# Layer 0 of a two-layer fp32 transformer: keys and values by seven half-size products, head dimension on partitions, turned by block transposes and memory

## What is computed

```
qkv  = silu(x @ qkv_w.T)            # per head q, k, v: 1024 x 128
for each chunk of tokens:
    scores = (q @ k.T) * diag_decay
    out    = scores @ v + (q * q_decay) @ state
    state  = state * chunk_decay + (k * k_decay).T @ v
xf   = out / sqrt(mean(out^2) + eps)
x    = layernorm(x + (sigmoid(x @ gate_w.T) * norm_w * xf) @ out_w.T)
```

## Time and profile before

| | us |
|---|---|
| median of three runs | 3062.18 (3061.16 to 3062.97) |
| profiled execution | 3054.36 |
| its span | 3052.4 |
| PE busy in the span | 2927.9 (96%) |
| DVE, ACT, POOL busy | 2027.4, 1544.3, 1740.4 |
| layer 0, head loop | until about 1112 |

### The profile page before, as it was taken

How to read it: one execution, slowest core, us unless ns; L and a number is a source line. 1 busy time by engine, 2 the same in 40 slices (tenths; PEclk the granted TensorE clock), 3 DMA queues, 4 the chain that set the end, 5 groups by cost and what they waited for, 6 DMA issues and landing times. The chain is left out here.

```text
span 3052.4 us, 57532 instructions
## 1 busy us (share of the span) xinstructions
PE 2927.9 (96%) x17440; PEld 2630.0 (86%) x17440; DVE 2027.4 (66%) x3231; ACT 1544.3 (51%) x3019; POOL 1740.4 (57%) x1300
## 2 busy tenths in 40 slices
PE   7999999999999978899999999999999999986998
PEld 6999999999999957799989899898989999975886
DVE  5555656555565556677777777777777777775555
ACT  4443443344344323566666666666666666663222
POOL 5554554455455432466665666666666666654664
PEclk9999999999999989999999999999999999998999
DMA  3222222222222220456666565665656666566541
GB/s 114 66 77 86 65 66 85 78 65 74 86 68 65 71 73 23 153 194 208 197 201 207 192 204 195 205 204 197 203 192 205 199 204 202 193 197 185 153 141 45
DMA packets 310074, 430.57 MB, mean 141 GB/s; under 512 B 30464, under 2 KB 237312, under 8 KB 309888
## 3 DMA queue, kind: packets, MB, share of 16 engines
q1 hardware_dynamic: 272336, 294.82, 32.5%
q10 hardware_dynamic: 37680, 135.02, 11.1%
HBM read 276.63 MB, written 153.09 MB: 141 GB/s over the span
## 5 line engine op out<-in xcount | busy, mean ns | idle before, releaser
L1588 ACT ACTIVATE b_prob<-b_s_ps,b_shift 128x1024 f32<-128x1024 f32 x256 | 285.7, 1116 | 345.9 <-DVE b_shift L1738 338.7
L82 PE MATMUL b_pj_kq<-b_w_hi,xT_hi 128*128 128x384 f32 x1008 | 351.7, 349 | 23.8 <-DVE b_nat L1714 22.5
L83 PE MATMUL b_pj_kq<-b_w_lo,xT_hi 128*128 128x384 f32 x1008 | 342.8, 340 | 0.0
L84 PE MATMUL b_pj_kq<-b_w_hi,xT_lo 128*128 128x384 f32 x1008 | 342.6, 340 | 0.0
L1744 DVE STREAM_TRANSPOSE b_blocks<-b_prob 128x1024 f32<-128x1024 f32 x256 | 317.4, 1240 | 29.0 <-ACT b_prob L1588 28.5
L489 POOL TENSOR_TENSOR a_ga_lo<-a_gated,a_ga_hi 128x512 fp32r<-128x512 f32 x64 | 112.8, 1763 | 366.7 <-ACT a_ga_hi L577 366.7
L1510 POOL TENSOR_TENSOR b_pT_lo<-b_pT_lo,b_pT_hi 128x1024 fp32r<-128x1024 f32 x128 | 304.9, 2404 | 18.7 <-ACT b_pT_hi L1577 18.6
L1510 POOL TENSOR_TENSOR pT_lo<-pT_lo,pT_hi 128x1024 fp32r<-128x1024 f32 x128 | 305.0, 2406 | 13.1 <-ACT pT_hi L1577 13.1
L1495 POOL TENSOR_TENSOR b_rstd<-b_mean_sq,power 128x4 f32<-128x4 f32 x128 | 128.8, 1007 | 320.1 <-DVE b_mean_sq L1724 313.5
L1738 DVE TENSOR_REDUCE b_shift<-b_s_ps 128x1 f32<-128x1024 f32 x256 | 307.1, 1200 | 1.7 <-PE b_s_ps L84 1.7
L82 PE MATMUL a_pj<-b_w_hi,xT_hi 128*128 128x256 f32 x1024 | 295.5, 289 | 13.2 <-DVE xT_lo L825 11.0
(11 more groups left out here) (302 smaller groups left out, 9149.3 us busy)
## 6 DMA issues: line engine op xcount, KB each, us to landing
bounce<-b_blocks ACTq DMA_DIRECT2D x256, 512.0 KB, 3.5
pT_lo<-bounce SPq DMA_DIRECT2D x512, 128.0 KB, 3.1
b_pT_lo<-bounce SPq DMA_DIRECT2D x512, 128.0 KB, 2.9
b_w_raw<-in_w SPq DMA_DIRECT2D x32, 768.0 KB, 5.8
b_w_raw<-in_w SPq DMA_DIRECT2D x95, 256.0 KB, 3.2
k_bounce<-a_k_blocks SPq DMA_DIRECT2D x32, 512.0 KB, 4.0
a_k_raw<-k_bounce SPq DMA_DIRECT2D x128, 128.0 KB, 2.9
a_w_raw<-in_w SPq DMA_DIRECT2D x32, 256.0 KB, 3.1
```

The costliest lines, as they stand in the source:

```text
L82: pe.matmul(out, w_hi, x_hi, start=first, stop=False, skip_group_check=partial)
L83: pe.matmul(out, w_hi, x_lo, start=False, stop=False, skip_group_check=partial)
L84: return pe.matmul(out, w_lo, x_hi, start=False, stop=last, skip_group_check=partial)
L1588: act.activation(prob[t % 2][:, :], s_ps[t % 2][:, :], ACT.Exp, bias=shift[:, t:t + 1], accum_out=row_sum[:, t:t + 1]).then_inc(exp_done, 1)
```

## The change

Keys and values are now also made by seven half-size products, at s = 0 to 3, with key weights as first and value weights as second row of the scheme (`PARTS`, pair `KV`; gate and queries are pair `QG`). Their weights get sums and partial splits of their own, on POOL and ACT at s = 4 to 6 of step h for head h+2. Keys and values come out with the head dimension on partitions, so the scores use `k_T` as it stands; both are turned to tokens on partitions for the updates and outputs: two block transposes, four writes to memory of 256 KB, one read of 1 MB, and ACT's `copy_v`. `decay_k` reads the moved blocks. At the start, the sums and splits of x are put in another order and the token sums are made earlier. The core of the diff:

```diff
 # SP
             def load_weights(h, t):
-                wait(sp, w_lo_done, NW * (h - 1) + (K_W + 1, V_W + 1, NW, NW)[t])
-                sp.dma_start(w_raw[t][:, :, :], w[ds(h, 1), t].rearrange("a p k d -> (a p) k d")).then_inc(w_in[t], 16)
+                wait(sp, w_lo_done, NW * (h - 1) + (L_S4, NW)[t // 2])
+                sp.dma_start(w_raw[t][:, :, :], w[ds(h, 1), t].rearrange("a p k d -> (a p) k d")).then_inc(
+                    w_in[t // 2], 16)
-            def move_k(g):
-                sp.wait_ge(k_blocked, g + 1)
-                sp.dma_start(k_bounce[:, :, :, :].rearrange("r p c n -> (r p) (c n)"),
-                             k_blocks[:, :, :, :].rearrange("p c t x -> p (c t x)")).then_inc(k_moved, 16)
-                sp.wait_ge(k_moved, MOVED * g + 16)
+            def move_kv(g):
+                sp.wait_ge(kv_blocked, 2 * g + 2)
                 for c in range(GROUPS):
-                    sp.dma_start(k_raw[c * BLK:(c + 1) * BLK].rearrange("p r t x -> p r (t x)"),
-                                 k_bounce[:, :, c, :].rearrange("r p n -> p r n")).then_inc(k_moved, 16)
+                    sp.dma_start(kv_bounce[:, :, c, :].rearrange("r x n -> x r n"),
+                                 kv_blocks[c * BLK:(c + 1) * BLK].rearrange("p r k t y -> p r (k t y)")).then_inc(
+                        kv_moved, 16)
+                sp.wait_ge(kv_moved, MOVED * g + WRITTEN)
+                wait(sp, v_copied, 2 * g)
+                wait(sp, k_decayed, 2 * g)
+                sp.dma_start(kv_raw[:, :, :, :, :].rearrange("p c k t y -> p (c k t y)"),
+                             kv_bounce[:, :, :, :].rearrange("r x c n -> (r x) (c n)")).then_inc(kv_moved, 16)
             def load(h, b):
                 load_weights(h, 0)
                 load_weights(h, 1)
                 load_output_weights(h - 2)
-                move_k(h - 2)
+                move_kv(h - 2)
                 load_weights(h, 2)
                 load_weights(h, 3)
                 load_decays(h - 1, 1 - b)
 # POOL, in step(h, ...), place s (at s == 6 half_out(h, b, 0) stands ahead of this)
-                    if split and s in SPLITS:
-                        split_lo(h + 2, SPLITS[s])
+                    for at, pair, g in ((s, QG, h + 1), (s - 4, KV, h + 2)):
+                        if (project, split)[pair == KV] and 0 <= at < 3:
+                            if at == 0:
+                                weight_sums(g, pair)
+                            for n in STAGES[at]:
+                                weight_low(g, pair, n)
 # STAGES = ((L_A1,), (L_S12, L_A22), (L_S3, L_S4)); weight_low(g, pair, n) waits for weight_high's of the same n
 # ACT
-            def copy_k(h, b, j):
...
+            def copy_v(h, j):
+                act.wait_ge(kv_moved, MOVED * (h + 1))
+                wait(act, attn, 2 * (h - 1) + j + 1)
+                cut = slice(CH * j, CH * (j + 1))
+                act.activation(v_nat[:, cut, :].rearrange("p t (c y) -> p t c y", y=BLK),
+                               kv_raw[:, :, 1, cut, :].rearrange("p c t y -> p t c y"), ACT.Copy).then_inc(v_copied, 1)
             def decay_k(h, b, j):
-                act.wait_ge(silu, 6 * h + 2 * j + 2)
+                act.wait_ge(kv_moved, MOVED * (h + 1))
...
+            def keep_first(g, bg, pair):
+                act.wait_ge(proj, NP * g + len(ORDER) * pair + P1)
+                wait(act, *((kv_blocked, 2 * g), (attn, 2 * (g - 1)))[pair])
+                act.activation(second(pair, bg)[:, 0:HALF], pj[pair][:, :], ACT.Copy).then_inc(kept, 1)
             def step(h, b, attention, project, output, split):
                 for s in range(NG):
                     if attention:
                         if s in (0, 2):
-                            copy_k(h, b, s // 2)
+                            copy_v(h, s // 2)
                             decay_k(h, b, s // 2)
...
+                    if project:
+                        sigmoids(h + 1, 1 - b, s)
+                    for at, pair, g in ((s, QG, h + 1), (s - 4, KV, h + 2)):
+                        if (project, split)[pair == KV] and 0 <= at < 3:
+                            for n in STAGES[at]:
+                                weight_high(g, pair, n)
 # PE
-                    if project and s < KV.stop:
-                        project_group(h + 1, s)
-                    if project and s >= KV.stop:
-                        for p in PRODUCTS[s]:
-                            product(h + 1, p)
+                    if project:
+                        for p in PRODUCTS[s % 4]:
+                            product(h + 1, s // 4, p)
 # in product(g, pair, p)
+                if p == P2:
+                    pe.wait_ge(kept, 2 * g + pair + 1)
 # DVE
+                    if project and s == 4:
+                        blocks(h + 1, 1 - b, 0)
+                        blocks(h + 1, 1 - b, 1)
+                    if project:
+                        projected(h + 1, 1 - b, s)
```

More of the change, by code:

```diff
@@ L434, in _ @@
             pool.memset(sh.power[:, :], -0.5).then_inc(zeroed, 1)
[L435 to L466, removed]
+            def raw(pair, row, cut):
+                return w_raw[PARTS[pair][row]][:, cut, :]
+            def weight_sums(g, pair):
+                pool.wait_ge(w_in[pair], 32 * (g + 1))
+                wait(pool, proj, NP * (g - 1) + len(ORDER) * (pair + 1))
+                to = {n: s_raw[pair][:, cut, :] for n, cut in in_s.items()}
+                done = 8 * g + 4 * pair
+                pool.tensor_tensor(to[S1], raw(pair, 1, LOWER), raw(pair, 1, UPPER), ALU.add).then_inc(w_summed, 1)
+                pool.tensor_tensor(to[S3], raw(pair, 0, LOWER), raw(pair, 1, LOWER), ALU.subtract).then_inc(w_summed, 1)
+                pool.wait_ge(w_summed, done + S1)
+                pool.tensor_tensor(to[S2], to[S1], raw(pair, 0, LOWER), ALU.subtract).then_inc(w_summed, 1)
+                pool.wait_ge(w_summed, done + S2)
+                pool.tensor_tensor(to[S4], raw(pair, 0, UPPER), to[S2], ALU.subtract).then_inc(w_summed, 1)
@@ L536, in _, with weight_high, tokens_high @@
         def _(act):
[L537 to L542, removed]
+            act.dma_start(w_raw[V_W][:, :, :], w[0, V_W]).then_inc(w_in[KV], 16)
             for k in (2, 3):
                 act.dma_start(xT_raw[k][:, 0:HALF], xT[k * P:(k + 1) * P, 0:HALF]).then_inc(x_in[0][k], 16)
[L545 to L548, removed]
+            def weight_high(g, pair, n):
+                act.wait_ge(w_in[pair], 32 * (g + 1))
+                wait(act, proj, NP * (g - 1) + len(ORDER) * (pair + 1))
+                if n == L_A1:
+                    t = PARTS[pair][0]
+                    hi, from_ = w_hi[t][:, :, :], w_raw[t][:, :, :]
+                elif n == L_A22:
+                    t = PARTS[pair][1]
+                    hi, from_ = w_hi[t][:, UPPER, :], w_raw[t][:, UPPER, :]
+                else:
+                    cut = {L_S12: slice(0, 4), L_S3: in_s[S3], L_S4: in_s[S4]}[n]
+                    hi, from_ = s_hi[pair][:, cut, :], s_raw[pair][:, cut, :]
+                    act.wait_ge(w_summed, 8 * g + 4 * pair + {L_S12: S2, L_S3: S3, L_S4: S4}[n])
+                act.activation(hi, from_, ACT.Copy).then_inc(w_hi_done, 1)
+            def tokens_high(*which):
+                for j, k in which:
                     cut = slice(j * HALF, (j + 1) * HALF)
@@ L593, in token_sums_high @@
-            def token_sums_high(*which):
-                for n in which:
-                    act.wait_ge(x_summed, 2 * n + 2)
-                    act.activation(t_hi[n], t_raw[n], ACT.Copy).then_inc(x_hi_done, 1)
-            def sigmoid(g, bg, s):
-                act.wait_ge(proj, NP * g + s + 1)
-                half = s % 2
-                wait(act, silu, 6 * g + s - 1 if s >= 2 else 6 * (g - 1) + 6 - s)
-                act.activation(sig_tmp[half][:, :], pj[half][:, :], ACT.Sigmoid).then_inc(sig, 1)
@@ L621, in query_sigmoid, with second @@
-            def query_sigmoid(g, bg, half):
-                act.wait_ge(combined, NC * g + (C21, C22)[half])
-                wait(act, silu, 6 * g + 3 + half)
-                act.activation(sig_tmp[half][:, :], q_T[bg][:, half * HALF:(half + 1) * HALF],
-                               ACT.Sigmoid).then_inc(sig, 1)
+            def second(pair, bg):
+                return (v_T, q_T[bg])[pair]
+            def keep_first(g, bg, pair):
+                act.wait_ge(proj, NP * g + len(ORDER) * pair + P1)
+                wait(act, *((kv_blocked, 2 * g), (attn, 2 * (g - 1)))[pair])
+                act.activation(second(pair, bg)[:, 0:HALF], pj[pair][:, :], ACT.Copy).then_inc(kept, 1)
@@ new lines, in sigmoid, with sigmoids @@
+            def sigmoid(g, silu_index, from_):
+                wait(act, silu, 6 * g + silu_index - 2)
+                act.activation(sig_tmp[(silu_index - 1) % 2][:, :], from_, ACT.Sigmoid).then_inc(sig, 1)
+            def sigmoids(g, bg, s):
+                pair = s // 4
```

(60 more changed lines are left out.)

315 lines of the change are left out of this document (132 added, 183 removed).

## The result

| | before | after |
|---|---|---|
| median, us | 3061.67 (3057.32 to 3062.97, 4 runs) | 3379.22 (3373.16 to 3382.17, 4 runs) |
| ratio | | 1.104, 95% interval 1.1021 to 1.106 |
| span of the profiled execution | 3052.4 | 3379.9 |
| one head in layer 0's loop | 33.48 | 44.3 |

The change makes the kernel 10.4% slower. The direction and the mechanism are the forecast ones; the size is not: 3276 was forecast. The time lies 39 us above the top of the forecast range (3340) and 4 us above the top of the wider one (3375).

The account below looks back on a forecast made before the run. Layer 0 was taken as bound by PE's matmuls, then by a ring of waits: 30 x 9.3 = +279, -58, -8, +2, total +215 on 3054.4, 3269 profiled, 3276 as median. Range 3215 to 3340 (0.65), wider 3185 to 3375.

Parts of the forecast that it names:

- Bound now, saved, beside it: Layer 0: matmuls bind; seven products save 1.8 us a head, 58 over 32 heads; added DVE, ACT, POOL work costs nothing.
- rival 1: Layer 0's loop: the move is in time and PE stays the bound; 2998 us, faster; chance 0.08.
- What is moved: SP's queue: the move of head H-2 now waits for POOL's last split at s = 6, stalling PE; 9.3 us a head.
- The ring: Per-head chain of waits through PE, ACT, POOL, SP and DMA between values-pair P2s: 41.0 us against 31.7 of PE work.
- PE, P2 to the end of the other pair's P2: PE's products, tiles, scores and the stretch from 525.37 to 534.77, at full clock: 18.0 us a head.
- low clock behind the stall: PE's matmuls run at the 1.2 GHz level after the stall: 1.5 us a head added.
- ACT and POOL, to the split's end: From PE's end through ACT's gate sigmoid and split, then POOL's jobs to S3 and S4: 7.3 us a head.
- SP and DMA, to the copy: From the split's end through a weight load, four writes and the 1 MB read: 12.3 us, between 9.3 and 15.2.
- ACT, to P2: ACT's copy_v, decay_k and keep_first with hand-overs, before PE's P2: 1.9 us a head.
- The times weighed beside the sum: Transfers by the skill's rule: loads and writes some 6 us, read 4.4, about 11 in place of 12.3; 3237 us.
- Rival 2: The same chain of waits but longer, through slow ga_lo and high-end transfers: 44.8 us a head, 3390 us; chance 0.12.
- The sum's other terms: No stall for the last two heads; head 0's old stall replaced, -8 us; start +2, between -3 and +6.

Follow-up runs that it names:

- e1: Changed kernel with the output weights and the move put ahead of the key and value weight loads in SP's queue; 3013.99 us, ratio 0.9862.
- e6: Changed kernel with 38 unread matmuls on PE in front of P2, inside the stall, none in head 30's step; 3312.3 us, ratio 1.0818.
- e4: Changed kernel with the move as one write of 1 MB and four reads of 256 KB; 3433.35 us, ratio 1.1236.
- e5: Changed kernel with SP's wait for POOL's last split kept ahead of the move, but the three weight loads not in front; 3283.43 us, ratio 1.0728.
- e2: Changed kernel with ACT's copy_v and decay_k at s = 2 and 3 in place of 0 and 2; 3177.19 us, ratio 1.0393.
- e3: Changed kernel with 32 unread matmuls on PE in front of P2, inside the stall; 3334.58 us, ratio 1.0904.

## Why the prediction was right and wrong

- **Bound now, saved, beside it.** Right in kind, and smaller in size. e1 shows the matmul part by itself: 33.48 to 32.03 us a head, 1.45 where 1.8 was forecast; its time gains 43 us where rival 1's sum has 64 (58 + 8 - 2). DVE's, ACT's and POOL's added work is covered but for the 0.17 us of one tile. The waits inside a pair cost nothing.
- **What is moved.** Right, and it is what decides: e1 removes it and 365 us go. Rival 1 (the move in time, 2998) is what e1 is, 3014; it needed the one order in SP's queue that the change does not have.
- **The ring, term by term**, forecast against the turn shown above:

| term | forecast | measured |
|---|---|---|
| PE, P2 to the end of the other pair's P2 | 18.0 | 18.2 (e1: 531.96 to 550.18) |
| low clock behind the stall | 1.5 | 2.6 (20.86 in all, 503.35 to 524.21) |
| ACT and POOL, to the split's end | 7.3 | 7.8 (to 532.0) |
| SP and DMA, to the copy | 12.3 | 13.75 (to 545.75) |
| ACT, to P2 | 1.9 | 1.8 |
| sum | 41.0 | 44.2 |

- **What failed** is the size of the ring's terms: 3.2 us a head too short, some 96 us on 30 heads. Two terms make 2.5 of the 3.2.
  - First the clock, "I add 1.5 us a head". It was read from the one stall of the kernel before, where the low level lasted 3.1 us behind the restart. Here it lasts 5.8 in the turn shown and 5.7 in the mean, and e6 prices it at 2.5. I gave this term one row and no upper end, while the transfers had both. The Trainium skill (TensorE: Matmul & The Clock Gate, Part 1) says that the number of slow matmuls behind a kernel's start varies from one run to the next. No kernel is traced twice here, but the traces show the like behind stalls: the low level lasts 4.2 to 6.2 us in the steps of the changed kernel and 3.1 to 6.2 in those of e4. One row could not show that spread, so the term needed bounds.
  - Second the writes, "Today's write took 4.1 with two loads ahead of it: 7.5": from the split's end to the read's issue took 8.9. That 4.1 was the time of a write of half the size. Four writes took 3.55 us to issue behind three loads (2.88 in e1 and e5), where I had 0.44 each from the reads of before, and from the first issue to the last landing 6.7. e4 shows that this is not their number (6.3 with one write), and e1 that it is mostly not the loads in front (6.2 without those of keys and values).
  - The read, from the one load of the same size, was right: 4.7 forecast, 4.8. POOL's S3 and S4 took 1.88 in place of 1.43; why is not shown.
  - The times weighed beside the sum, 6 us for loads and writes and 4.4 for the read, add up to some 10.5, which the prediction rounds to 11; they took 8.7 (532.18 to 540.92) and 4.8.
- **Rival 2** (the ring, longer: 3390) comes within 11 us of the time, but by luck: it has 0.9 for ga_lo, which kept its 1.27, and 2.9 for the transfers, which grew by 1.45, and nothing for the clock.
- **The sum's other terms.** No stall for heads 30 and 31 holds: the last distance between two copies of P1, 1345.70 to 1377.88, is 32.2 us. The start does not: it was put at +2, with +6 as the most. PE begins at 10.19, but waits 7.6 us for the low part of a token sum in front of its second product:
```profile
20.70 0.77 PE L82 MATMUL a_c_ps<-x_store,e_lo 128*128 128x512 f32 x1 [7.61 <-DVE x_store L836]
```
```profile
49.80 1.05 PE L740 MATMUL a_s_ps<-a_q_T,a_k_T 128*128 128x128 f32 x8
```
The first scores start at 49.80, where the kernel before would have been ready at 41.29 (47.48 less its stall of 6.19): 8.5 us later, and some 10 with what head 0's products save. With the ring's 96 us that is about the 103 us between forecast and time.

## What to carry to other kernels

When a step is made of in-order queues, look for the ring before summing engine time: write down for each moved transfer what stands ahead of it in its queue and what stands behind its wait on the other side; here an edit of four lines in SP's order turned a loss of 10.4% into a gain of 1.4%. Splitting weights later is free for the engines and not for the queue that waits for the split. A term of a ring counts in full on each turn, however idle its engine is, so each needs an upper end, the clock behind a stall too; and a transfer is costed from one of its own size.

## What the runs showed of the hardware

- The length of a stall alone did not tell whether PE's granted clock would fall. In e2 it fell behind a stall of 2.5 us in every step from 100 us on; in e3 it fell behind 11 of 28 stalls of 1.8 to 3.2 us, behind one of 1.83 and not behind one of 2.50. In e6, from 107 us on, it never fell in the loop behind stalls of up to 1.7 us.
- Nor did it tell for how long the clock stayed low once PE worked again: 3.1 us behind a stall of 6.2, 3.4 in e2, 4.2 to 6.2 behind stalls of 9.1 to 11.3 in the changed kernel, 3.1 to 6.2 behind stalls of 10.7 to 13.8 in e4.
- Unread matmuls in a stall made the kernel 67 us faster (e6).
- 1 MB read from memory as four transfers in pieces of 2 KB took 7.8 us, as one in pieces of 8 KB 4.8; the write of 1 MB was 6.3 us as one transfer and 6.7 as four.
